# Moving the low-part subtractions of seven late token rows from VectorE to GpSimd in a float32 self-attention stage

## What is computed

```python
x = _layernorm(x + _L0_ffn_ref(x, ...))            # the rows that come in
# S, B, H = 112 tokens x 16 sequences x 1024; 8 groups, each 4 query heads, one key, one value, of width 128
qkv = jnp.einsum('sbh,ph->sbp', tokens, weight_qkv)
...
scores = jnp.einsum('bhsd,bhtd->bhst', q, k) * scale
scores = jnp.where(causal, scores, jnp.finfo(scores.dtype).min)
attn = jax.nn.softmax(scores, axis=-1)
out = jnp.einsum('bhst,bhtd->bhsd', attn, v)
return jnp.einsum('sbe,he->sbh', out, weight_proj)
```

## Time and profile before

| what | value |
|---|---|
| median of three runs | 3239.0 us (3230.96 to 3241.22) |
| the profiled execution: its own time, its span | 3240.99 us, 3239.0 us |
| busy: PE, DVE, ACT, POOL | 3025.5, 1983.3, 1591.9, 1157.6 us |
| mean granted clock of PE | 0.969 of full speed |
| the self-attention products, first to last | 871 to 2480 us |
| the rounds with a late row (G = 1 to 7) | 949.1 to 1720.3 us |

### The profile page before, as it was taken

How to read it: one execution, slowest core, us unless ns; L and a number is a source line. 1 busy time by engine, 2 the same in 40 slices (tenths; PEclk the granted TensorE clock), 3 DMA queues, 4 the chain that set the end, 5 groups by cost and what they waited for, 6 DMA issues and landing times. The chain is left out here.

```text
span 3239.0 us, 69982 instructions
## 1 busy us (share of the span) xinstructions
PE 3025.5 (93%) x26232; PEld 2522.1 (78%) x26232; DVE 1983.3 (61%) x4938; ACT 1591.9 (49%) x4162; POOL 1157.6 (36%) x1023
## 2 busy tenths in 40 slices
PE   5999999996699999999989999999999699999997
PEld 3888888874488888788878888888887578888886
DVE  6788888884545455545554444444445588888885
ACT  2777877783432323232323222232222487777774
POOL 2222222212264554454536564555644101111110
PEclk8999999996699999999999999999999799999999
DMA  9777877763012222222254121221211855656651
GB/s 280 188 188 188 198 195 188 192 148 91 20 53 88 79 83 69 76 79 82 87 217 146 63 85 60 72 72 54 85 59 63 270 146 151 151 151 151 151 146 47
DMA packets 234199, 397.96 MB, mean 123 GB/s; under 512 B 32281, under 2 KB 161913, under 8 KB 233354
## 3 DMA queue, kind: packets, MB, share of 16 engines
q1 hardware_dynamic: 230408, 391.29, 43.2%
q10 hardware_dynamic: 3458, 2.20, 0.2%
HBM read 296.98 MB, written 96.43 MB: 121 GB/s over the span
## 5 line engine op out<-in xcount | busy, mean ns | idle before, releaser
L1460 POOL TENSOR_TENSOR sa_r_lo<-sa_raw,sa_r_hi 128x512 fp32r<-128x512 f32 (+1 forms) x304 | 466.1, 1533 | 679.4 <-ACT sa_r_hi L1754 595.5
L756 ACT ACTIVATE L_probs<-L_masked,L_least 112x375 f32<-112x375 f32 x1024 | 628.1, 615 | 79.5 <-DVE L_least L885 75.4
L885 DVE CUSTOM_DVE_ANT_0 L_masked<-L_scores,L_nmask 112x375 f32<-112x375 f32 x1024 | 552.6, 544 | 175.2 <-PE L_scores L489 139.0
L494 PEld LDWEIGHTS L_turned<-ident_sb,L_probs 112*125 112x125 f32 x3072 | 457.1, 189 | 107.0 <-issue 48.1
L494 PE MATMUL L_turned<-ident_sb,L_probs 112*125 112x112 f32 x3072 | 526.3, 280 | 7.1 <-ACT L_probsT L751 3.5
L1597 PE MATMUL sa_banks<-both_hi,sa_r_hi 128*128 128x420 f32 (+1 forms) x1344 | 498.5, 371 | 11.4 <-DVE both_lo L1930 6.6
L1597 PE MATMUL sa_banks<-both_lo,sa_r_hi 128*128 128x420 f32 (+1 forms) x1344 | 490.5, 365 | 0.0
L1597 PE MATMUL sa_banks<-both_hi,sa_r_lo 128*128 128x420 f32 (+1 forms) x1344 | 490.3, 365 | 0.0
L1996 DVE TENSOR_TENSOR sa_acc<-sa_acc,sa_banks 128x512 f32<-128x512 f32 x448 | 304.6, 685 | 246.3 <-PE sa_banks L1656 240.3
L489 PE MATMUL L_scores<-L_krep,L_qrep 128*112 128x376 f32 x1024 | 418.0, 409 | 7.5 <-DMA L_qrep<-query_parts 6.5
L751 ACT COPY L_probsT<-L_turned 125x336 f32<-125x336 f32 x768 | 337.5, 440 | 177.1 <-PE L_turned L494 169.6
(11 more groups left out here) (320 smaller groups left out, 5322.4 us busy)
## 6 DMA issues: line engine op xcount, KB each, us to landing
L_qrep<-query_parts SPq DMA_DIRECT2D x256, 224.0 KB, 6.2
sa_raw<-in_wqkvU_dram SPq DMA_DIRECT2D x192, 256.0 KB, 3.3
L_krep<-ctx_parts SPq DMA_DIRECT2D x256, 188.0 KB, 4.2
sa_raw<-in_wprojU_dram SPq DMA_DIRECT2D x128, 256.0 KB, 3.0
query_parts<-L_qT_hi SPq DMA_DIRECT2D x64, 224.0 KB, 6.4
query_parts<-L_qT_lo SPq DMA_DIRECT2D x64, 224.0 KB, 7.0
L_xcur<-x SPq DMA_DIRECT2D x64, 224.0 KB
L_val<-in_ctx_dram SPq DMA_DIRECT2D x64, 187.5 KB
```

The source lines that it names most:

```text
L494: mm = pe.transpose(turned[0:TC, m % 2, S * j:S * j + S], probs[0:S, m % 4, TC * j:TC * j + TC], ident[0:S, 0:S])
L756: nc.scalar.activation(probs[0:S, e % 4, :], masked[0:S, e % 4, :], ACT.Exp, bias=least[0:S, e:e + 1], scale=-1.0, accum_out=rsum[0:S, e:e ...
L885: v.tensor_tensor_reduce(out=masked[0:S, n % 4, :], in0=scores[0:S, (NH * t + n) % 3, 0:T], in1=nmask[0:S, :], scale=1.0, scalar=HUGE, op0 ...
L1460: p.tensor_tensor(lo, src, hi.bitcast(F32), ALU.subtract).then_inc(done, 1)
```

## The change

The low parts of the late rows are made by POOL in place of DVE: four in the Q01 pair of rounds 1 to 7, after POOL has made the fourth weight of that pair, and three after the fourth weight of the KV pair of the next round (in round 7, ahead of `heads(7, 1)`). DVE forms the differences of the second batch in chunk 1 of the projection instead of chunk 0, and waits before each batch of differences for POOL's low parts of the batch before.

```diff
+            def late_low_parts(r, i):
+                for n, o in enumerate(ROUNDS[i]):
+                    pool.wait_ge(hi_ok, made(1, r, i) + n + 1)
+                    hi, lo = operand_place(1, r, o)
+                    p.tensor_tensor(lo, operand_source(1, r, o), hi.bitcast(F32), ALU.subtract).then_inc(lo_ok, 1)
...
                 elif G:
-                    weights(G, KV)
+                    weights(G, KV, 0, RING)
+                    if late_row(G - 1) is not None:
+                        late_low_parts(late_row(G - 1), 1)
+                    weights(G, KV, RING)
...
-                weights(G, Q01)
+                weights(G, Q01, 0, RING)
+                if late_row(G) is not None:
+                    late_low_parts(late_row(G), 0)
+                weights(G, Q01, RING)
...
                 if ends_half(G):
+                    if late_row(G) is not None:
+                        late_low_parts(late_row(G), 1)
                     heads(G, 1)
...
-                    if hp == 0 and c == 0 and late_row(G) is not None:
+                    if hp == 0 and c == 1 and late_row(G) is not None:
+                        dve.wait_ge(lo_ok, made(1, late_row(G), 1))
                         differences(1, late_row(G), 1)
-                    if hp == 0 and c == 1 and late_row(G) is not None:
-                        low_parts(1, late_row(G), 1)
...
                 if r is not None:
+                    dve.wait_ge(lo_ok, made(1, r, 0))
                     differences(1, r, 0)
-                    low_parts(1, r, 0)
```

More of the change, by code:

```diff
@@ L1924, in differences, with low_parts @@
                 dve.drain()
[L1926 to L1930, removed]
+            def low_parts(c):
+                for n, o in enumerate(MAKE):
+                    dve.wait_ge(hi_ok, OPS * c + n + 1)
+                    hi, lo = operand_place(0, c, o)
+                    v.tensor_tensor(lo, operand_source(0, c, o), hi.bitcast(F32), ALU.subtract).then_inc(lo_ok, 1)
             def combine(G, pr, which):
@@ L2047, in _ @@
                 if c >= 2:
-                    low_parts(0, c - 2)
+                    low_parts(c - 2)
             for c in range(NC - 2, NC):
                 differences(0, c)
-                low_parts(0, c)
+                low_parts(c)
             dve.wait_ge(hi_ok, OPS * NC)
```

## The result

The changed kernel takes 3248.19 us (median of 8 runs, 3244.98 to 3256.44) against 3238.01 us for the kernel before (8 runs, 3230.96 to 3241.33). The ratio is 1.0034, with a 95% interval from 1.0022 to 1.0046: slower by about 11 us, just past the 10 us that the prediction called the limit of telling. It lies inside the range given (3232 to 3254), 5 us above the value (3243).

A forecast was written before the change was run, and what follows sets the result against it. TensorE (PE) was taken to set the time, busy 102.82 of 104.90 us in round 3. Terms -6.6 - 0.7 + 15.8 - 5.0 gave +3.5 us on 3240.99, so a median of about 3243 us, range 3232 to 3254.

The forecast's parts named there:

- The wait before T3: Q01 pair, rounds 1 to 7: TensorE idles 2.0 us before the product needing the fifth weight, queued behind late low parts.
- GpSimd's idle time before the first late low part: Q01 pair: sign that GpSimd stands idle about 2.3 us, waiting for the first high part.
- The last projection weight: End of GpSimd's queue in the Q01 pair: this weight reaches TensorE 0.2 to 0.3 us late.
- After Q23: Projection after Q23, rounds 1 to 6: moved differences leave a 0.6 us wait, gaining 1.1 us a round, -6.6 us.
- the opening of the prediction: Waits on `sa_acc`, rounds 1 to 7: 21.0 us is all that taking work from VectorE can win.
- In round 7: Second batch: three low parts leave VectorE beside softmax work, and small waits go, -0.7 us.
- After Q01: Projection after Q01: Q23 weights arrive earlier relative to TensorE, so 5.0 of 6.0 us of waits go.
- The clock: Rival: the new wait drops TensorE to half rate, about 1.7 us lost a round, 3250 to 3255 us; chance 0.19.
- The sum: All terms together: +3.5 us on the profiled execution; chance 0.68 that it comes as summed.
- Its own signs: Listed checks: 2 us wait, GpSimd pieces and idle time, smaller `sa_acc` waits, granted clock 1.00, rounds 1 to 6 within 1 us.
- the two largest terms: Q01 pair's new waits, +15.8 us over seven rounds, and the gain after Q23, -6.6 us over six.
- the third: Projection after Q01: gain from Q23 weights arriving earlier relative to TensorE, -5.0 us.

The follow-up runs named there:

- experiment 5: The changed kernel measured again with no further edit, beside the kernel before; ratio to the kernel before 1.0021.
- experiment 6: The changed kernel plus eight unused 128x128 transposes on TensorE before its wait for the fifth weight in the Q01 pair; ratio to the kernel before 1.0029.
- experiment 11: The changed kernel with SyncE's stores of the first batch put after the loads of the Q23 weights; ratio to the kernel before 1.0017.
- experiment 1: The changed kernel with the first batch of low parts back on VectorE, only the second on GpSimd; ratio to the kernel before 0.9978.
- experiment 2: The changed kernel with only the first batch on GpSimd, the second on VectorE with differences in chunk 0; ratio to the kernel before 1.0056.
- experiment 3: The changed kernel with the Q01 pair's late low parts behind the fifth weight instead of the fourth; ratio to the kernel before 0.9989.
- experiment 4: The kernel before, all low parts on VectorE, with the second batch's differences in chunk 1 and low parts in chunk 2; ratio 0.9981.
- experiment 9: The kernel before with one edit: SyncE's stores of the first batch put after the loads of the Q23 weights; ratio 0.9977.
- experiment 7: From experiment 1, with two of the first batch's four low parts on GpSimd behind the fourth weight; ratio to the kernel before 0.9995.

## Why the prediction came out as it did

**The mechanism was right, step by step.** The wait before T3 was forecast as 2.0 us in all seven rounds, from fixed pieces; it is 1.95 to 1.98 in rounds 2 to 7, and 1.30 in round 1. That the pieces are fixed did not hold in later executions, where a late landing made the wait up to 2.95 us (experiments 5, 6 and 11). Experiments 1, 2 and 3 show that this wait, by the order on GpSimd, is the loss: without the first batch there it is gone, with it alone it is whole, and with the fifth weight put ahead of the late low parts it is gone too, and 3.0 us of waits are left behind it. GpSimd's idle time before the first late low part was forecast as 2.3 us and is 2.35, its piece at 0.73 (from a row of 112x256) and is 0.734 in the mean of the 28 that read `sa_dif`; the 21 that read `sa_late` took 0.864, since some of them met a subtraction of VectorE (the first of round 3 took 1.01 us). The last projection weight was forecast 0.2 to 0.3 us late: the stretch from T3 to the projection went from 8.00 to 8.27 us at full clock.

**After Q23** the new wait was put at 0.6 us, between 0.15 and 0.9, and is 0.80 to 0.96: a gain of 1.0 to 1.16 us a round in the lengths, for 1.1 forecast. The working for this part names the place of the differences, and experiment 4 shows that in rounds 1 to 6 this is the whole of it. Ahead of the additions of chunk 1 they held a bank that TensorE wanted at once; ahead of those of chunk 2 a weighing lies between. What experiment 4 corrects is the opening of the prediction, which speaks of taking work from VectorE as what wins these waits: none had to be taken. In round 7, 0.2 us were gained for the 0.7 forecast.

**After Q01** the gain was counted as 5.0 us and is 3.8 (waits of 2.1 us left of 6.0). A term mis-sized by 1.2 us. The cause of the waits was named rightly: experiment 9 takes all of them away by putting the loads first.

**The clock** was a rival with a chance of 0.19, priced at nothing in the sum. It came in two of seven rounds in one profile and five in the other, at 1.3 us each (9.58 or 9.59 less 8.27), where the rival had 1.7. Here is the largest miss: 2.6 us of the 7.3 in the first profile. Experiment 6 kept the clock up and won no time by it, so the net cost is likely less; how much less lies below what these runs can tell.

**The sum**, for rounds 1 to 7 of the profiled execution: forecast +3.5, found +7.3. The differences are 2.6 for the clock, 1.2 after Q01, 0.6 after Q23 and in round 7, and 0.5 less for the wait before T3 with what hangs on it; together 3.9, which is the whole difference but for rounding. Over runs the change costs 11 us in one comparison and 7 in the other, so up to a few us more than that profile shows. The profiled execution was the fastest of its eight runs. Experiment 5's waits of 2.4 and 2.8 us and its five slow stretches show in what way other runs are longer. That they make up all of the rest was not shown.

**Its own signs.** Of what the prediction said would show it right or wrong, the wait before T3 and GpSimd's pieces and idle time came as said. Three did not: the waits after Q01 fell to 2.1 us and not to nearly nothing, the granted clock was under 1.00 in round 6 (0.92 over its Q01 pair), and rounds 3, 4 and 6 are 1.2, 1.7 and 2.7 us longer than before, not within 1 us. In rounds 3 and 4 the kernel before waited only 0.40 and 0.19 us after Q01, so there was nearly nothing to win against the new wait. Round 6 had no such wait before and has the lower clock as well.

So the answer "about the same, a little slower" held, but by more luck than margin: the two largest terms were right within a tenth, the third was a quarter too large, and all three nearly cancel, so that a term left at zero can decide on which side of 0.3% the result lies.

## What to carry to other kernels

When work moves to an engine that is half idle, look for what stands behind it in that engine's queue, and how long the piece waits for its own input. Here an engine 50% busy held up the bound by 2 us a round, since a wait for the high part was put ahead of a weight that had 2.6 us in hand; one place further down, the same work made the Q01 pairs 5 us longer instead of 17. And before moving work between engines, try moving it in time on its own engine (here that gave the whole gain in rounds 1 to 6, and a loss in round 7), and ask which queue the late input comes from: putting SyncE's loads ahead of its stores gave as much as the good half of the change.

## What the runs showed of the hardware that was not expected

- TensorE, in a steady stream of products, did not always keep its 2.4 GHz behind one idle stretch of about 2 us. Of the 24 waits before T3 between 1.88 and 2.95 us in four profiles (the change twice, experiments 2 and 11), 13 were followed by a stretch at 1.2 GHz (granted clock 0.50 to 0.70 over the next 5 us). None of the 12 waits of 1.68 to 1.78 us after Q23 in the kernel before and in experiment 2 was. Of five others above 2 us, the last projections of round 7 left out, those of 2.06 us (experiment 9) and 2.46 us (experiment 2, after Q01) were, and those of 2.01, 2.11 and 2.35 us (experiments 5, 6 and 7) were not. The Trainium skill, TensorE: Matmul & The Clock Gate, What's actually happening, has the rate of an idle engine at half. The slow stretches agree: in round 4 of experiment 5 the granted clock was 0.66 over 5 us. The runs show besides that whether a wait of this size is hit varies from execution to execution of one kernel.
- Keeping the clock up with eight idle transposes brought no time back (ratio 1.0029 against 1.0021, intervals overlapping), although a lower-clock stretch from T3 to the projection is 1.2 to 1.3 us longer (experiments 5 and 6; 2.4 us in round 3 of experiment 11).
- GpSimd's 128x1024 piece of 2.58 us held up a VectorE subtraction of 128x256 that began 0.3 us behind it until its own end: 2.58 us in place of 0.42 (experiment 4). The Trainium skill, SBUF — State Buffer, SBUF: two separate sides, calls the shared ports an exclusive lock for a whole instruction; by that rule the size of the piece that one meets is the price, and the trace agrees.
